# Pre-LayerNorm transformer layer: the statistics of two LayerNorms moved from the epilogue into the attention loop

## The reference, cut to what matters

```
h  = layernorm(x)                                # no scale, no shift, eps 1e-5
q, k, v = split(h @ attn_w.T + attn_b)           # 16 heads of 64
p  = softmax over k of (k.q / 8, masked so that k <= q)
x  = x + (p v) @ out_w.T + out_b
h  = layernorm(x)
s  = h @ Win + bin                               # 64 values a token
g  = sum over 16 of relu(s*W1 + b1) * W2, + b2   # 64 values a token
x  = x + g @ Wout + bout
```

## Time and profile before

| what | us |
|---|---|
| two timed executions | 4363.54 and 4456.43, median 4409.98 |
| profiled execution, its own time | 4348.28 |
| its span, slowest core (core 1) | 4346.4 |
| spans of the 8 cores | 4321.7 to 4346.4 |
| mean granted TensorE clock | 0.756 to 0.759 of full |
| busy: PE, ACT, DVE, POOL | 2779.7, 1803.0, 1111.3, 100.3 |

### The profile page before, as it was taken

One profiled execution on the slowest core, in us unless ns is written; L12 is line 12 of the kernel. 1 busy time (PEld: TensorE's weight loads), 2 busy tenths in 40 slices (PEclk: granted clock), 3 DMA queues, 4 the chain that ended last, 5 costly groups with the idle time before them and its releaser, 6 DMA issues.

```text
span 4346.4 us, 39831 instructions; the slowest of 8 cores (4321.7 to 4346.4 us)
## 1 busy us (share of the span) xinstructions
PE 2779.7 (64%) x12288; PEld 1070.4 (25%) x12288; DVE 1111.3 (26%) x2486; ACT 1803.0 (41%) x2945; POOL 100.3 (2%) x196
## 2 busy tenths in 40 slices
PE   0657576586656658577674756757666475765874
PEld 0223232232222223222231312223222132322321
DVE  3141321401324141230223224032131413214112
ACT  0414337166141624517523261643733234272481
POOL 0000000000000000000000000000000000000000
PEclk9868688698676868768776776878877676776885
DMA  7010000100101010010000001000000000000000
GB/s 197 13 37 18 23 30 15 44 6 15 39 20 39 15 34 15 15 39 10 20 30 30 30 20 39 10 20 29 15 25 27 32 25 25 30 15 30 10 10 25
DMA packets 36933, 121.98 MB, mean 28 GB/s; under 512 B 7610, under 2 KB 7738, under 8 KB 36732
## 3 DMA queue, kind: packets, MB, share of 16 engines
q0 software_dynamic: 19456, 67.12, 4.4%
q1 hardware_dynamic: 17020, 51.80, 4.1%
q10 hardware_dynamic: 256, 0.52, 0.0%
HBM read 85.34 MB, written 34.08 MB: 27 GB/s over the span
## 4 chain that ended last, share of the span: by engine, by line
PE 48%; ACT 17%; DVE 11%; issue 11%; DMA 10%; ACTq 1%; DVEq 0%; POOLq 0%; SPq 0%
PE P L314 10%; PE P L389 10%; ACT s_probs L361 7%; PE P L441 6%; PE P L291 6%; DMA s_zz<-zscr 5%; PE P L352 5%; DMA zscr<-s_zz 3%; ACT s_zz L407 3%; ACT s_zz L404 3%; DVE s_xln L219 2%; DVE s_x L452 2%; DVE s_probs L484 2%; PE P L536 2%; PE P L540 2%
## 5 line engine op out<-in xcount | busy, mean ns | idle before, releaser
L361 ACT ACTIVATE s_probs<-P 128x1024 bf16<-128x1024 f32 (+3 forms) x1280 | 1062.6, 894 | 399.2 <-PE P L356 353.1
L389 PE MATMUL P<-s_probs,s_vaug 128*65 128x512 bf16 (+3 forms) x2560 | 719.0, 397 | 198.2 <-DVE s_comb L421 109.1
L352 PE MATMUL P<-s_q,s_k 64*128 64x512 bf16 (+3 forms) x1280 | 465.1, 391 | 429.1 <-ACT s_probs L361 394.6
L369 DVE TENSOR_TENSOR s_probs<-s_probs,s_tril 128x256 bf16<-128x256 bf16 x512 | 145.9, 292 | 1397.2 <-ACT s_probs L361 1394.6
L441 PE MATMUL P<-s_ow,s_comb 128*128 128x512 bf16 x1024 | 338.0, 489 | 246.6 <-DVE s_comb L421 207.0
L356 PE MATMUL P<-s_q,s_k 64*128 64x512 bf16 (+3 forms) x1280 | 474.5, 398 | 0.0
L314 PE MATMUL P<-s_xlnT,s_wqk 128*128 128x512 bf16 x2048 | 444.8, 379 | 0.0
L389 PEld LDWEIGHTS P<-s_probs,s_vaug 128*65 128x65 bf16 x2560 | 246.5, 119 | 564.6 <-issue 468.6
L237 ACT ACTIVATE s_stats<-s_stats 128x1 f32<-128x1 f32 x128 | 37.7, 295 | 780.8 <-DVE s_stats L234 780.8
L421 DVE TENSOR_TENSOR s_comb<-P,s_zz 64x512 bf16<-64x512 f32 x256 | 175.0, 684 | 671.0 <-DMA s_zz<-zscr 667.0
L473 PE MATMUL P<-s_id,s_xln 128*128 128x128 bf16 x512 | 108.4, 258 | 370.4 <-ACT s_probs L480 276.3
(11 more groups left out here) (58 smaller groups left out, 2001.6 us busy)
## 6 DMA issues: line engine op xcount, KB each, us to landing
s_x<-x SPq DMA_DIRECT2D x64, 512.0 KB, 3.7
s_zz<-zscr POOLq DMA_DIRECT2D x128, 256.0 KB, 3.5
out<-s_x POOLq DMA_DIRECT2D x64, 512.0 KB, 2.9
s_x<-wqk_t SPq DMA_DIRECT2D x16, 512.0 KB, 7.4
s_x<-wv_t SPq DMA_DIRECT2D x8, 512.0 KB, 6.3
s_x<-ow_t SPq DMA_DIRECT2D x8, 512.0 KB, 6.4
zscr<-s_zz ACTq DMA_DIRECT2D x128, 4.0 KB
s_x<-bias_rows SPq DMA_DIRECT2D x1, 260.0 KB
```

What stands on the lines that cost most here:

```text
L352: s.op("pe", lambda E, c=hp, k=kt, c0=col0, S=SC: E.matmul(S[:, c0:512], s_k[0:64, c * T + k * 128: c * T + (k + 1) * 128], s_q[0:64, c * ...
L361: texp = s.op("act", lambda E, S=SC, pb=prb, c0=col0: E.activation(pb[:, :].rearrange("p (h c) -> p h c", h=2, c=512)[:, :, c0:512], S.rea ...
L369: dep_pv = s.op("dve", lambda E, pb=prb, c0=col0: E.tensor_tensor(pb[:, :].rearrange("p (h c) -> p h c", h=2, c=512)[:, :, c0:c0 + 128], p ...
L389: P=pv_banks[bank]: E.matmul(P[:, c0:512], s_vaug[:, ti * NH * 65 + hh2 * 65: ti * NH * 65 + hh2 * 65 + 65], pb[:, hi2 * 512 + c0: hi2 * 5 ...
```

## The change

`emit_ln` is cut in two: `emit_ln_stats` (sum of squares, sum, the three column instructions) and `emit_ln_apply` (Ln and Exp on ACT, the last column instruction and the normalised tile on DVE). `phaseA_ln` likewise: its first half also issues the load of x. `attention` takes a hook that is called behind each unit; behind units 0 and 1 it issues the load and the statistics of tiles 0 and 1 of the next stage. The second half of tile 0 stands where LN(0) stood; that of tile 1 stands behind epilogueA(1), ahead of TR(0,1), where LN(1) had stood behind epilogueB(0). LN(2) and LN(3) stay. The variance instruction gets one more dependency, on ACT's last use of the same columns. Lines from L219 on are numbered differently in the changed kernel: L219 is L221 there, L224 L226, L234 L236, L237 L244, L243 L251, L246 L254, L276 L299, L369 L392, L421 L444, L452 L477, L484 L509, L544 L569.

```diff
--- before.py
+++ after.py
@@ -212,9 +212,11 @@
             "v_evac": None,
             "pv_done": {0: None, 1: None, 2: None, 3: None},
             "txl": {},
+            "lnA_act": {},
+            "ln_pend": {},
         }
 
-        def emit_ln(src, dst_xln, scol, dep_src, dep_xln_war, sum_tok=None):
+        def emit_ln_stats(src, dst_xln, scol, dep_src, dep_xln_war, sum_tok=None):
             cS, cQ, cM, cMS, cVV, cR, cNR = (scol + j for j in range(7))
             tsq = s.op("dve", lambda E: E.scalar_tensor_tensor(
                 dst_xln[:, :], src[:, :], 1.0, src[:, :], ALU.mult, ALU.mult,
@@ -233,13 +235,19 @@
                 deps=[tm])
             tv = s.op("dve", lambda E: E.scalar_tensor_tensor(
                 s_stats[:, cVV:cVV + 1], s_stats[:, cQ:cQ + 1], 1.0 / 1024.0,
-                s_stats[:, cMS:cMS + 1], ALU.mult, ALU.subtract), deps=[tsq, tms])
+                s_stats[:, cMS:cMS + 1], ALU.mult, ALU.subtract),
+                deps=[tsq, tms, st_["lnA_act"].get(scol)])
+            return tsq, tv
+
+        def emit_ln_apply(src, dst_xln, scol, tsq, tv):
+            cS, cQ, cM, cMS, cVV, cR, cNR = (scol + j for j in range(7))
             tsr = s.op("act", lambda E: E.activation(
                 s_stats[:, cR:cR + 1], s_stats[:, cVV:cVV + 1], AF.Ln,
                 bias=s_stats[:, 63:64]), deps=[tv])
             trc = s.op("act", lambda E: E.activation(
                 s_stats[:, cR:cR + 1], s_stats[:, cR:cR + 1], AF.Exp,
                 scale=-0.5), deps=[tsr])
+            st_["lnA_act"][scol] = trc
             tnr = s.op("dve", lambda E: E.scalar_tensor_tensor(
                 s_stats[:, cNR:cNR + 1], s_stats[:, cM:cM + 1], -1.0,
                 s_stats[:, cR:cR + 1], ALU.mult, ALU.mult), deps=[trc])
@@ -248,16 +256,31 @@
                 ALU.mult, ALU.add), deps=[tnr, tsq])
             return txl
 
-        def phaseA_ln(sq, g, i, slot, extra_deps=()):
+        def emit_ln(src, dst_xln, scol, dep_src, dep_xln_war, sum_tok=None):
+            tsq, tv = emit_ln_stats(src, dst_xln, scol, dep_src, dep_xln_war,
+                                    sum_tok)
+            return emit_ln_apply(src, dst_xln, scol, tsq, tv)
+
+        def phaseA_ln_stats(sq, g, i, slot, extra_deps=()):
             tile = g * GT + i
             tk = s.dma("sp", f"ch_x{slot}", s_x[slot][:, :],
                        x_h[sq, tile * 128:(tile + 1) * 128, :],
                        deps=[st_["out_dma"].get(slot)] + list(extra_deps))
             xs = i % 2
-            xln = s_xln[xs]
-            txl = emit_ln(s_x[slot], xln, 8 * i, tk, st_["xln_read"][xs])
+            stats = emit_ln_stats(s_x[slot], s_xln[xs], 8 * i, tk,
+                                  st_["xln_read"][xs])
+            st_["ln_pend"][i] = (slot, stats)
+
+        def phaseA_ln_apply(i):
+            slot, (tsq, tv) = st_["ln_pend"][i]
+            xs = i % 2
+            txl = emit_ln_apply(s_x[slot], s_xln[xs], 8 * i, tsq, tv)
             st_["x_read"][slot] = txl
             st_["txl"][i] = txl
+
+        def phaseA_ln(sq, g, i, slot, extra_deps=()):
+            phaseA_ln_stats(sq, g, i, slot, extra_deps)
+            phaseA_ln_apply(i)
 
         def phaseA_tr(i, half=None):
             xs = i % 2
@@ -327,7 +350,7 @@
             st_["qk_evac"] = qk_evac
             st_["v_evac"] = v_evac
 
-        def attention(sq, g):
+        def attention(sq, g, hook=None):
             nkt = (g + 1) * GT
             qk_evac = st_["qk_evac"]
             v_evac = st_["v_evac"]
@@ -425,6 +448,8 @@
                         st_["pv_done"][bank] = tcm
                         comb_written.append(tcm)
                     st_["zz_read"][pi] = comb_written[-1]
+                if hook is not None:
+                    hook(u)
             st_["P1_freed"] = comb_written[-1]
             st_["P2_freed"] = comb_written[-1]
             return comb_written
@@ -559,7 +584,6 @@
             phaseA_tr(i)
         phaseA_qkv(*stages[0])
         for idx, (sq, g) in enumerate(stages):
-            comb = attention(sq, g)
             nxt = stages[idx + 1] if idx + 1 < len(stages) else None
             slot = lambda i: (idx * GT + i) % 6
             nslot = lambda i: ((idx + 1) * GT + i) % 6
@@ -568,17 +592,27 @@
                 if nxt is not None:
                     phaseA_ln(nxt[0], nxt[1], i, nslot(i))
 
+            def hook(u):
+                if u < 2 and nxt is not None:
+                    phaseA_ln_stats(nxt[0], nxt[1], u, nslot(u))
+
+            comb = attention(sq, g, hook)
+
+            def LNA(i):
+                if nxt is not None:
+                    phaseA_ln_apply(i)
+
             def TR(i, half=None):
                 if nxt is not None:
                     phaseA_tr(i, half)
 
-            LN(0)
+            LNA(0)
             epilogueA(sq, g, 0, slot(0), comb)
             TR(0, 0)
             epilogueA(sq, g, 1, slot(1), comb)
+            LNA(1)
             TR(0, 1)
             epilogueB(sq, g, 0, slot(0))
-            LN(1)
             epilogueA(sq, g, 2, slot(2), comb)
             TR(1, 0)
             epilogueB(sq, g, 1, slot(1))
```

## The result

| | before | changed |
|---|---|---|
| median of the timed executions | 4351.27 us (10) | 4401.36 us (11) |
| ratio, with its 95% interval | 1 | 1.0111 (1.0081 to 1.0142) |
| profiled execution, its own time | 4348.28 | 4392.44 |
| span, slowest core | 4346.4 (core 1) | 4390.6 (core 7) |
| spans, mean of the 8 cores | 4334.5 | 4382.2 |

The change costs 1.1%, and the interval is clear of 1. The median and the ratio are taken over more executions than the two that stood before the prediction, and the ratio leaves disturbed ones out.

The account below looks back on a forecast made before the run. Taken to be bound by a chain of hand-offs, no engine near full. Nothing gained in the epilogue, 25.4 us lost in the attention and 14.9 us in the epilogue: 40.3 us on 4355.9, so 4396 us, range 4352 to 4452.

Parts of the forecast that it names:

- What bounds the kernel: Whole kernel: no engine near full, PE busy 64% and DVE 26%; a chain of hand-offs between engines and DMAs.
- Parts 1 and 2: LayerNorm work leaving the epilogue's start and middle: DVE then waits for the out-projection anyway, so each is worth 0.
- Part 3: Statistics behind the combines of units 0 and 1: at g = 0 masks move 3.18 us, 8 times, 25.4 us; elsewhere hidden.
- Part 4: Tile 1's Ln/Exp and DVE pair ahead of epilogueB(0): DVE's later copy counts, 15 x 0.99 = 14.9 us.
- The clock: Out-projections of tiles 2 and 3: fast or slow halves dealt anew, 19 us less to 17 us more, either equally likely.
- The sum: Whole kernel: 0 + 0 + 25.4 + 14.9 = 40.3 us, put on 4355.9 us, giving 4396 us, 0.9% slower.
- The chances: Whole kernel's time: within 2% 0.90, slower by more 0.08, faster by more 0.02; the forecast itself 0.72.
- 1 (faster): Epilogue LayerNorms were on the path: up to 3.15 us at each of 30 places, net 4302 us; chance 0.05.
- 3 (every stage pays): Attention: statistics delay P·V or masks in every stage, 110 us, 4466 us, slower by over 2%; chance 0.05.
- 2: Attention hides its statistics too, so only the pair ahead of epilogueB(0) is paid: 4371 us; chance 0.06.
- 4, the clock against it: Out-projections: all 7 fast ones turn slow, 17 us more, 4421 us, up to 4450 by the median; chance 0.12.

Follow-up runs that it names:

- the kernel with both costs undone in place: Changed kernel with the statistics ahead of the combine and tile 1's second LayerNorm half behind epilogueB(0); ratio to the kernel before 0.9981.
- the kernels with one half each: Kernel before plus, ahead of epilogueB(0), an unused Ln and Exp on ACT (ratio 1.0015) or two unused DVE instructions (ratio 1.0001).
- the last kernel: Kernel with epilogueA split and statistics ahead of the combine, plus the next tile's residual add and LayerNorm inside epilogueB; ratio to the kernel before 0.9257.

## Why the prediction was right or wrong

*What bounds the kernel:* right. Busy times stayed and the 44 us came nearly all from waits.

*Parts 1 and 2, worth 0:* right, shown by the kernel with both costs undone in place (0.9981) and by DVE's wait of 236.2 us instead of 98.8. DVE's idle time before the add of tile 0 (L452, now L477) grew to 5.92 us in the first stage and 5.0 to 6.3 us in the 15 (5.3 forecast), before that of tile 2 to 7.35 us and 5.9 to 7.5 (7 forecast).

*Part 3, 25.4 us:* right. 3.10 us an insertion, 24.8 us in the two stretches, nothing to speak of at g of 1 to 3 and nothing ahead of unit 3. Of PE's wait I had said 9.1 us; it was 8.70, since PE came to it 0.3 us later.

*Part 4, 14.9 us:* the mechanism was right, with 0.99 us and the later of two copies deciding, both seen in the rows and in the kernels with one half each. The term was mis-sized: from the L452 of tile 1 to tile 3 it was 18.4 + 2.3 = 20.7 us.

*The clock:* here a step failed. The sum gave the clock nothing, with the reason that the result was "as likely below as above". It measured 5.8 us, all to one side. Of the 20.7 us, 14.9 are the pair; the other 5.8 go with the out-projections of tiles 2 and 3, which were less often fast: 13 of 120 at tile 2 instead of 64. Their second halves alone account for 4.4 us of it (2.25 us in the mean before and 2.40 now at tile 2, 2.13 and 2.27 at tile 3, in 15 stages of the six cores with complete records). All three kernels with 0.86 to 0.99 us of delay show it. Why the sort depends on the delay stays open. The rule of the Trainium skill that I drew on, in "TensorE: Matmul & The Clock Gate", Part 1, gave no reason for a side, and the trace does not agree with what I concluded from it: with chances equal for every shift the counts 64, 13 and 75 would not come out of delays of 0, 0.99 and 2.2 us.

*The sum:* 40.3 us were forecast, 47.7 us of mean span and 44.2 us of the profiled executions came. 4396 us against 4401.36, a rise of 0.9% against 1.1%. That the time came out within 6 us is in part luck: I had put the sum on 4355.9 us, and the median of before came out at 4351.27, so that the base was 5 us too high where the cost was too low.

*The chances:* here the second step failed, the one from the sum to the forecast. The sum said slower, with all costs of one sign and both gains at nothing, yet 0.90 went to "within 2%", with the reason that a measurement tells about 2% from no change. That reason was wrong: the interval came out at 0.3% to either side, and the rise of 1.1% is clear of it. A forecast of +0.9% with a range of its own of 4380 to 4415 us was a forecast of a slower kernel and should have been given as one: every value in that range was above the base of 4355.9 us.

*Rivals:* 1 (faster) and 3 (every stage pays) did not happen; the idle rows that spoke against them held. 2 was excluded by the attention's 24.8 us. 4, the clock against it, happened in part: 5.8 us of the 17 that all slow would have cost.

## What to carry to other kernels

Before moving work off an engine, read what ends its next wait: the engine was idle 0.9 to 2.5 us behind these LayerNorms, and freeing it gave idle time. Before moving it elsewhere, find the instruction queued behind the new place and who waits for it: ahead of the combine the statistics were free, four instructions later they cost 3.1 us each time at g = 0. And the same edit can be worth nothing or 50 us by what the order around it lets DVE do at that time; here most of the gain of the last kernel (7.4%, 313 us by the profiled executions) lay in the order of the epilogue, and about 50 us of it in the statistics.

## What the runs showed of the hardware that I had not expected

The share of out-projections of tile 2 that ran their whole second half at the 2.4 GHz level depends on the delay ahead of them, and not monotonically. In a fast one the granted clock is 1.00 there (802.20 to 804.10 us in the kernel before), in a slow one 0.68 (274.40 to 277.00 us), since it rises only on the way. The counts are 64 of 120 fast with none, 13 with 0.99 us, 75 (and 1 slow) with 2.20 us. And one instruction of 128x1024, float32 in and bf16 out, delayed DVE by 0.60 us where it read no scalars from s_stats (0.68 us long), less than the 0.73 us from L246 to its follower (0.81 us long).
